# An early-fusion network of two layers: attention of layer 0 on folded matrices, other passes for its norms, and a new order of all stages

## The reference

```python
h = patchify(x) @ W + b                              # 16 batches of 36 image tokens, 64 channels
h = concat([h, table[x_txt] + pe], axis=1)           # and 512 text tokens: 548 tokens a batch
# layer 0, attention
u = layernorm(layernorm(h)) * g + b                  # the second with gain and bias
Q, K, V = u @ wq + bq, u @ wk + bk, u @ wv + bv
R = layernorm(h) + relu(Q @ K.T / 8) @ V
h = h + layernorm(R + relu(R @ w1 + b1) @ w2 + b2) * fg + fb
# layer 0, MoE: 8 experts, each token to its best, at most 1.25 * T / 8 tokens an expert
z = layernorm(h); probs = softmax(z @ gate_w + gate_b)
h = h + prob_best * kept * (relu(z @ w1[e] + b1[e]) @ w2[e] + b2[e])
# layer 1, attention over channels: 16 heads of 4, k and v normalised in each head
z = layernorm(h); q, k, v = split(z @ W_qkv.T + b_qkv)
a = gelu((q @ (k.T @ v / 548) + z) @ W_proj + b_proj) + z
h = h + a
# layer 1, MoE: each token through all 8 experts, the two best weighted
z = layernorm(h); w = top2(softmax(z @ Wr + br))
h = h + sum_e w_e * (gelu((norm(z) * ln_g[e] + ln_b[e]) @ W1[e] + b1[e]) @ W2[e] + b2[e])
```

## Time and profile before

| | |
|---|---|
| median of 3 runs | 848.64 us (847.61 to 850.04) |
| span of the profiled execution (no other time of it is given) | 846.4 us |
| PE busy | 729.7 us, 86% |
| DVE busy | 612.2 us, 72% |
| ACT busy | 481.7 us, 57% |
| POOL busy | 433.1 us, 51% |

### The profile page before, as it was taken

How to read it: one execution, slowest core, us unless ns; L and a number is a source line. 1 busy time by engine, 2 the same in 40 slices (tenths; PEclk the granted TensorE clock), 3 DMA queues, 4 the chain that set the end, 5 groups by cost and what they waited for, 6 DMA issues and landing times.

```text
span 846.4 us, 15831 instructions
## 1 busy us (share of the span) xinstructions
PE 729.7 (86%) x4619; PEld 487.1 (58%) x4619; DVE 612.2 (72%) x2308; ACT 481.7 (57%) x980; POOL 433.1 (51%) x470
## 2 busy tenths in 40 slices
PE   3589999999988689965789989989989999899995
PEld 1366777666655257643456555556555656566672
DVE  4557899989678536576777889888888977786231
ACT  1255655555541146642246877766788666777552
POOL 5732617773764600246646667667676763223222
PEclk8599999999997889995679999999999999999988
DMA  7910000000000023220022221222221122223200
GB/s 216 359 53 9 14 8 19 22 21 5 5 4 3 4 58 97 75 66 12 6 57 57 62 56 17 57 59 63 62 63 41 31 55 61 62 62 61 62 14 7
DMA packets 60976, 43.69 MB, mean 52 GB/s; under 512 B 29100, under 2 KB 56252, under 8 KB 60636
## 3 DMA queue, kind: packets, MB, share of 16 engines
q1 hardware_dynamic: 51820, 36.35, 17.2%
q0 software_dynamic: 7200, 4.17, 2.4%
q10 hardware_dynamic: 1872, 2.18, 0.9%
HBM read 31.66 MB, written 13.47 MB: 53 GB/s over the span
## 4 chain that ended last, share of the span: by engine, by line
PE 26%; ACT 15%; DVE 14%; issue 9%; POOL 2%; DMA 1%; DVEq 0%; ACTq 0%; POOLq 0%
ACT scratch L715 7%; PE psum L628 6%; PE psum L1140 5%; PE psum L1141 4%; ACT L715 3%; PE psum L1340 3%; ACT L664 2%; PE psum L1147 2%; DVE xt L788 1%; PE psum L1322 1%; PE psum L1118 1%; PE psum L602 1%; ACT L659 1%; DVE kh L885 1%; DVE stats L1507 1%
## 5 line engine op out<-in xcount | busy, mean ns | idle before, releaser
L715 ACT ACTIVATE scratch<-psum,fb 128x512 f32<-128x512 f32 (+2 forms) x288 | 172.2, 665 | 37.4 <-PE psum L1141 36.1
L628 PE MATMUL psum<-scratch,w_fw 128*64 128x256 f32 (+2 forms) x1152 | 141.7, 383 | 11.4 <-DVE scratch L978 5.7
L538 POOL TENSOR_TENSOR prob<-prob,scratch 128x256 f32<-128x256 f32 (+2 forms) x126 | 79.3, 629 | 141.0 <-DVE scratch L978 139.4
L497 POOL DMA_INDIRECT uu<-expert_out,slot_i x80 | 83.2, 1040 | 88.3 <-issue 68.7
L1079 POOL DMA_INDIRECT slots_buf<-xt,slot_i x80 | 82.5, 1032 | 68.0 <-DVE slot_i L1754 45.8
L628 PEld LDWEIGHTS psum<-scratch,w_fw 128*64 128x64 f32 x1152 | 79.1, 140 | 56.5 <-DVE scratch L978 13.5
L1065 POOL DMA_INDIRECT emb<-in_table,w_ids x64 | 63.4, 991 | 55.8 <-DVE stats L1507 33.5
L1405 ACT ACTIVATE prob<-psum 128x292 f32<-128x292 f32 (+1 forms) x160 | 55.1, 396 | 52.2 <-PE psum L1207 52.1
L1140 PE MATMUL psum<-kh,fw_hi 128*128 128x512 f32 x176 | 80.0, 455 | 0.6 <-ACT scratch L715 0.5
L1141 PE MATMUL psum<-kh,fw_lo 128*128 128x512 f32 x176 | 71.8, 408 | 0.0
L978 DVE SCALAR_TENSOR_TENSOR scratch<-psum,w_fb,X 128x256 f32<-128x256 f32 (+1 forms) x119 | 54.4, 460 | 16.9 <-PE psum L628 15.5
(11 more groups left out here) (272 smaller groups left out, 1715.7 us busy)
## 6 DMA issues: line engine op xcount, KB each, us to landing
X<-share_buf SPq DMA_DIRECT2D x32, 512.0 KB
slots_buf<-zeros SPq DMA_DIRECT2D x8, 352.0 KB, 4.9
expert_out<-zeros SPq DMA_DIRECT2D x8, 352.0 KB, 4.9
out<-H SPq DMA_DIRECT2D x16, 128.0 KB
X<-in_patches ACTq DMA_DIRECT2D x3, 576.0 KB, 7.3
slots_buf<-xt,slot_i POOLq DMA_INDIRECT x80, 2.2
uu<-expert_out,slot_i POOLq DMA_INDIRECT x80, 2.5
emb<-in_table,w_ids POOLq DMA_INDIRECT x64
```

Source lines behind the costliest of these rows:

```text
L497: pool.indirect_dma_start(yg[b % 2][0:rows, s, :], None, expert_out, bass.IndirectOffsetOnAxis(slot_i[0:rows, b, (s + 1) % SLOTS:(s + 1) % ...
L538: pool.tensor_tensor(total[t % 2][:, 0:z], total[t % 2][:, 0:z], part[m % PARTS][:, 0:z], ALU.add).then_inc(sem("summed"), 1)
L628: last = pe.matmul(bank(6 + n % 2)[h * D:(h + 1) * D, 0:z], w["fw2"][:, e * J + j, :], hid[(J * n + j) % (J * UNITS)][:, h * z:(h + 1) * z ...
L715: act.activation(hid[m % (J * UNITS)][:, 0:z], bank(2 + m % 4)[:, 0:z], ACT.Gelu, bias=fb1[:, e * J + j:e * J + j + 1]).then_inc(sem("gelu ...
```

## The change

- `norm1b` writes the normalised tokens plus one (the mean taken is lowered by the deviation), twice: DVE writes one copy, ACT's `twin` the other beside it. Four tiles `xt` instead of two. Since the 64 channels of such a token sum to 64, a bias divided by 64 can be added to each row of a weight; so `prep` makes of query and key weights one matrix `w_u`, and of the value weights and bias `w_v`.
- `t1` turns the five slots of 128 columns (both copies) into the WIDE banks; `k_high` and `k_low` make the halves of the turned tokens themselves: they are the keys. `q` is `w_u` against both halves, four fp32r matmuls. `k`, `v`, `vals`, `stack1` are gone. `attend` multiplies the scores with the tokens, and `o_turn` is the product with `w_v`.
- `norm2a` ends with five scalar_tensor_tensor (subtract mean, times gain), one a slot; `norm2b` is the reciprocal and five scalar_tensor_tensor. `norm3b` leaves out the subtraction of the mean; the gate's weights and the experts' first weights are centred instead (`centre_w`, `centre_copy`).
- The attention weights come in one DMA (`wqkv`, 48 KB) instead of three.
- All tables of the order are new. `moe_bias` stands third on PE, `moe_gains`, `low_moe`, `high_moe`, `high_w`, `low_w` among batches 0 to 3; the gathers stand earlier, the scatters later on POOL; sixteen fills more stand at the end of stage one and the start of the experts; of the later fills ten stand behind `kv` of batch 0. `up` of the first tile stands right behind the first `route`; `kv_b` of batch 0 stands before `mixed` of batch 1.

```diff
             def t1(b):
-                banks.take(pe, TURN, sem("xs1"), b + 1)
-                pe.wait_ge(sem("norm1b"), (b + 1) * PER["norm1b"] - 1)
-                turn_pairs(pe, xt[b % 2], 0).then_inc(sem("t1"), 1)
+                banks.take(pe, WIDE, sem("k_low"), b + 1)
+                pe.wait_ge(sem("twin"), b + 1)
+                for s in range(SLOTS):
+                    rows, at0 = P if s < TXT else N_IMG, s // 2 * P
+                    last = pe.transpose(bank(2 + s % 2)[:, at0:at0 + rows], xt[b % XT][0:rows, s].rearrange("p k c -> p (k c)"), ident[0:rows, 0:rows])
+                last.then_inc(sem("t1"), 1)
...
             def q(b):
-                q_or_k(b, "wq")
-            def k(b):
-                q_or_k(b, "wk")
-            def v(b):
-                slots_by(pe, bank(7), xs1[b % 2], w["wv"]).then_inc(sem("v_prod"), 1)
+                banks.take(pe, WIDE, sem("q_low"), b + 1)
+                pe.wait_ge(sem("k_low"), b + 1)
+                for h, z in enumerate(SIDES):
+                    pe.matmul(bank(2 + h)[:, 0:z], w_u[:], kh[b % 2][:, h * ODD:h * ODD + z], start=True, stop=False)
+                    last = pe.matmul(bank(2 + h)[:, 0:z], w_u[:], kl[b % 2][:, h * ODD:h * ODD + z], start=False, stop=True)
+                last.then_inc(sem("q_prod"), 1)
...
-                turn_back(pe, ot[b % 2], 1).then_inc(sem("o_turn"), 1)
+                slots_by(pe, bank(1), ot[b % 2], w_v).then_inc(sem("o_turn"), 1)
...
+            def centre_w(c):
+                pe.matmul(bank(0), centre[:], ew1[0:D, c * 512:(c + 1) * 512], start=True, stop=True).then_inc(sem("centre_prod"), 1)
...
+            def twin(b):
+                act.wait_ge(sem("norm1b"), b * PER["norm1b"] + 5)
+                if b >= XT:
+                    act.wait_ge(sem("t1"), b - XT + 1)
+                act.activation(xt[b % XT][:, :, 1, :], xt[b % XT][:, :, 0, :], ACT.Identity).then_inc(sem("twin"), 1)
...
             def norm1b(b):
+                st(dve.tensor_tensor(mean1[:], mv1[b % 2][:, :, 0], sd1[b % 2][:, 1, :], ALU.subtract))
...
+                st(dve.tensor_tensor(zt[:], H[:, b], bc(mean1[:], D), ALU.subtract))
+                st(dve.tensor_tensor(ratio1[:], sd1[b % 2][:, 1, :], rs[:, 0, :], ALU.mult))
+                st(dve.tensor_tensor(x, zt[:], bc(rs[:, 1, :], D), ALU.mult))
+                st(dve.scalar_tensor_tensor(out=X[:, b], in0=x, scalar=-1.0, in1=bc(ratio1[:], D), op0=ALU.add, op1=ALU.mult))
...
             def norm2a(b):
+                for s in range(SLOTS):
+                    st(dve.scalar_tensor_tensor(out=uu[b % 2][:, s, :], in0=uu[b % 2][:, s, :], scalar=mv2[b % 2][:, s, 0:1], in1=w["fg"][:], op0=ALU.subtract, op1=ALU.mult))
...
             def norm2b(b):
-                st(dve.tensor_tensor(zt[:], uu[b % 2][:], bc(mv2[b % 2][:, :, 0], D), ALU.subtract))
-                st(dve.tensor_tensor(zt[:], zt[:], bc(rs[:, 0, :], D), ALU.mult))
-                st(dve.tensor_tensor(zt[:], zt[:], bs(w["fg"][:], SLOTS), ALU.mult))
-                st(dve.tensor_tensor(H[:, b], H[:, b], zt[:], ALU.add))
+                for s in range(SLOTS):
+                    st(dve.scalar_tensor_tensor(out=H[:, b, s, :], in0=uu[b % 2][:, s, :], scalar=rs[:, 0, s:s + 1], in1=H[:, b, s, :], op0=ALU.mult, op1=ALU.add))
...
             def norm3b(b):
-                st(dve.tensor_tensor(zt[:], H[:, b], bc(mv3[b % 2][:, :, 0], D), ALU.subtract))
-                st(dve.tensor_tensor(xt3[b % XT3][:, 0:SLOTS, :], zt[:], bc(rs[:, 0, :], D), ALU.mult))
+                st(dve.tensor_tensor(xt3[b % XT3][:, 0:SLOTS, :], H[:, b], bc(rs[:, 0, :], D), ALU.mult))
```

More of the change, by code:

```diff
@@ L57 @@
 FMAX = 3.4028234663852886e38
-PER = dict(norm1a=11, norm1b=4, qk_low=3, vals=1, resid=1, norm2a=11, norm2b=5, norm3a=10, norm3b=3, gate=6, place=7,
+PER = dict(norm1a=11, norm1b=6, resid=1, norm2a=16, norm2b=6, norm3a=10, norm3b=2, gate=6, place=7,
            mixed=12, weighted=5, norm4=3, kvnorm=3, fold=3, resid2=11, norm5=4, route_a=11, route_b=6)
@@ L259, in early_fusion_kernel @@
[L259 to L263, removed]
+        POOL_ONE = ((-50.75, "gather_a"), (-38.625, "gather_b"), (84.5, "offset"), (320.75, "scatter_a"), (354.25, "scatter_b"))
@@ L264, in early_fusion_kernel @@
+        DVE_ONE = ((2.25, "norm1a"), (44.5, "norm1b"), (109.625, "k_low"), (123.375, "q_low"), (183, "resid"), (229.375, "norm2a"),
+                   (241.625, "norm2b"), (245.625, "norm3a"), (254.25, "norm3b"), (262.375, "gate"), (277.098, "place"))
         MOE, DOWN_LAG, GELU_LAG, WEIGH_LAG, SUM_LAG, BACK_LAG, FINISH_LAG = 170, 1.5, 0.75, 2.5, -0.5, 12.75, 12
@@ L1171, in _ @@
             pe.wait_ge(sem("early_in"), EARLY_IN)
-            pe.matmul(bank(7)[:, 0:1], w["wq"][0:D, 0:P], w["norm_b"][:], start=True, stop=True)
-            pe.matmul(bank(7)[:, 1:2], w["wk"][0:D, 0:P], w["norm_b"][:], start=True, stop=True)
-            pe.matmul(bank(7)[:, 64:64 + D], w["norm_b"][:].to_broadcast([D, P]), w["wv"][0:D, 0:D], start=True, stop=True).then_inc(sem("bias_prod"), 1)
+            pe.wait_ge(sem("affine"), 1)
+            turned = [aff[:, m].rearrange("p k c -> p (k c)") for m in range(3)]
@@ L1629, in q_low @@
                 lo = by_side(qst[b % 2][D:P, :], RIGHT)
-                dve.scalar_tensor_tensor(out=lo, in0=both(2)[D:P], scalar=bq[D:P, 0:1], in1=lo.bitcast(F32), op0=ALU.add, op1=ALU.subtract).then_inc(sem("qk_low"), 1)
-            def k_low(b):
-                dve.wait_ge(sem("qk_high"), 2 * b + 2)
-                hi, lo = by_side(kh[b % 2][:], RIGHT), by_side(kl[b % 2][:], RIGHT)
-                dve.scalar_tensor_tensor(out=lo, in0=both(2), scalar=bk[:, 0:1], in1=hi.bitcast(F32), op0=ALU.add, op1=ALU.subtract).then_inc(sem("qk_low"), 2)
@@ L1637, in vals @@
[L1637 to L1641 removed]
+                dve.tensor_tensor(lo, both(2)[D:P], lo.bitcast(F32), ALU.subtract).then_inc(sem("q_low"), 1)
             def resid(b):
@@ L1755, in place @@
                 st.close()
-            table = dict(resid=resid, q_low=q_low, norm1a=norm1a, norm2a=norm2a, gate=gate, norm3b=norm3b, k_low=k_low, vals=vals, norm1b=norm1b, norm2b=norm2b,
+            table = dict(resid=resid, q_low=q_low, norm1a=norm1a, norm2a=norm2a, gate=gate, norm3b=norm3b, k_low=k_low, norm1b=norm1b, norm2b=norm2b,
                          place=place, norm3a=norm3a, prep=prep, late_weights=late_weights, moe_gains=moe_gains, low_moe=low_moe)
```

492 lines of the change are left out of this document (376 added, 116 removed), and 113 rows, old and new, of tables (ACT_MOVED, DVE_MOVED, PE_MOVED).

## The result

The changed kernel takes 799.42 us (median of 4 runs, 798.7 to 799.72) against 849.34 us of the kernel before (4 runs): a ratio of 0.941, 95% interval 0.939 to 0.943. That is 50 us less where 27.5 were forecast. The profiled executions have spans of 797.9 and 846.4 us, 48.5 us apart.

| milestone | before, us | after, us | gained in this stretch |
|---|---|---|---|
| first copy of attended tokens | 48.45 | 54.53 | -6.1 |
| the copy of batch 15 | 249.89 | 241.15 | 14.8 |
| last placing | 286.72 | 273.74 | 4.2 |
| first product of the experts | 298.51 | 286.63 | -1.1 |
| kv bias of batch 0 | 379.08 | 359.47 | 7.7 |

What follows compares the result with a forecast made beforehand. Stage one was taken as bound by PE and DVE together, layer 1 mainly by PE. From 848.64 us: -15 pace, -6.5 stage-one end, 0 start, +1 between stages, -4 and -3 stage two, -27.5 to 821; range 797 to 838, own 811 to 827.

Steps and rivals of the forecast that it cites:

- Pace of stage one: Stage one, per batch: DVE relieved by 1.0 us and PE by 1.75, pace 13.43 to 12.4, -15 us over 15 batches.
- norm 2: DVE in stage one: ten 128x64 pieces at 0.15 us replace four passes, -0.45 us a batch, bounds -0.5 and +0.8.
- the pace follows the smaller relief: Stage one: with PE and DVE both full, the pace falls by DVE's 1.0 us a batch, not PE's 1.75.
- rival C: Stage one: norm 2's pieces cost 0.28 us each, pace stays DVE-bound at 13.4, -15 is lost, 836 us; chance 0.07.
- the sign that DVE would be fuller than PE: Stage one: DVE fuller than PE in the new profile, listed among what would show the forecast.
- Once-only work: MoE bias folding, gains and low half move from stage one's end to batches 0 to 3: -5.5 us, costed at nothing there.
- Between the stages: Before the experts: clock-keeping matmuls after the last count grow from 30 to 60, +1 us, bounds 0 and +5.
- Stage two: Layer 1 beside its MoE, steady part: new order, no work removed, 14 more table loads; -3 us, between -25 and +18.
- the -4 at the head: Start of stage two: kv of batch 0 first, up product a batch earlier, fills clumped; -4 us, bounds -12 and +6.
- Rival B: Stage two: new order closes PE's idle time, 22.7 to 23.7 us a batch instead of 25, total 799 to 810; chance 0.22.
- My own sign of being wrong: Layer 1: pitch outside 24.0 to 25.2 us a batch; also stage one paced by POOL or a chain of waits.
- Rival D: Stage two slower: clumped fills and earlier MoE leave PE thin at the head, loads delay gelus; 852 us, chance 0.08.

Runs made afterwards that it cites:

- The experiment in the old order: The changed kernel with stage one in the order of the kernel before, new steps fitted into the old places; 883.01 us, ratio 1.040.
- the exchanges: All four engines' stage-two lists and fills swapped: changed kernel with the old order, 833.15 us; kernel before with the new order, 812.87 us.
- the three moves that I tried alone: Kernel before, two weighings earlier on DVE: 890.94 us; kernel before, square later on ACT: 862.87 us; changed kernel, square earlier on ACT: 810.74 us.
- theory 1: Expectation of 789 to 793 us for the changed kernel with the last bias added by DVE instead of POOL; measured 797.0 us.

## Why the forecast was right in direction, and too small

**Pace of stage one.** Forecast 12.4 us, -15; measured 12.44, -14.8. The number held, but its terms did not, so that it held is luck. Between the copies of batches 5 and 14 DVE works 109.8 us before and 105.7 after, 12.20 and 11.75 us a batch: a relief of 0.45 instead of 1.0. The term that was mis-sized is norm 2: the pieces take 0.21 each, 1.07 us for five twice, against my 0.15, so the exchange gives +0.2 instead of -0.45 (my bounds were -0.5 and +0.8), and with it my sum would be -0.34. In this stretch the pace fell by 1.03 us (13.79 to 12.76); the other half is idle time of DVE, 1.6 us a batch before and 1.0 after, for which the forecast had no term. That the pace follows the smaller relief of work is therefore not what happened: the batches got shorter by more than DVE's relief and by less than PE's, which is 1.4 us (13.20 to 11.77) and not 1.75. The order is the likely giver of the other half; no run separates it. That rival C would make the pace 13.4 was wrong all the same, and so was the sign that DVE would be fuller than PE (92.2 and 92.5).

**The arithmetic needs its order.** I took the pace from the engines' sums and a chain of waits only as a way to be wrong. The experiment in the old order shows that chain at 18.3 us a batch, with the new steps at the places I gave them. This was not in the forecast. The old arithmetic in the new order of stage one was not run.

**Once-only work.** Forecast -5.5 up to the last placing and, with -1 for scatters and +1 for fills, 0 from there to the experts; measured -4.2 and +1.1. It was costed at nothing at the start, and that failed: 2.07 us for each of four centring products, where I had taken 0.5 from a bf16 matmul of as many columns, and three of them on the way of batch 0. The bias products take 6.96 us instead of the 4.37 of before (granted clock 0.50 from 23 to 30 us, 0.83 at 266.5 to 271 before), but lie in PE's wait for q's low half. The first copy came 6.1 us late (bound +4). It mattered little: without this work the total is 1.9 us less.

**Between the stages.** +1 forecast, 1.1 measured; 60 at 0.24 each end at 286.8, and against thirty they hold the experts' first product back by 2.3 us. What they keep is the clock in the experts (1.00 instead of 0.83 from 280 to 300 us), worth 1.9 of that.

**Stage two.** The step that failed is "between -25 and +18 I take -3, near nothing, for no work is removed", with the -4 at the head. Measured: -7.7 at the head (bound -12), 0.0 until batch 5, and -28.9 from there to the end. The -7.7 lie between the experts' first product and the first kv bias, where I had 0 for the experts; PE works 70.2 us there instead of 74.9, at a clock of 1.00 instead of 0.97. For all of it the exchanges give 34 and 36 us. Rival B was this case, 22.7 to 23.7 us a batch for 14 to 25 us; it got 0.22, and the pitch measured is 23.4. My own sign of being wrong, a pitch outside 24.0 to 25.2, came with it. The argument against it, that only 9 of PE's 23 idle us had one cause, counted waits by the last releaser. PE's idle time had several releasers, and the order of all four lists took it from 25.4 to 14.8 us in eleven batches; the other 7.2 us of the gain there are busy time that shrank with the same products. Which entries do it stays open: the three moves that I tried alone, two in the old order and one in the new, each made the kernel slower, by 11 to 42 us, and neither of those in the old order hit the changed place exactly.

**Table loads.** 14 more were forecast and 14 came: 74 loads of 1.283 us in the trace against 60. ACT's share in the ten batches rose from 73 to 84%, and PE waited 4 us in them for gelus (L1466 2.7, L954 1.3), so most of the 18 us was hidden. By the Trainium skill ("ScalarE: Activation LUTs", section "What ACT_TABLE_LOAD costs") a drain of about 1.38 us would come on top of each; no run here shows it, since in the changed kernel too the next operation (566.66 us) starts 1.29 us after the load began (565.37). Rival D had part of its condition (a clump of fills, a clock of 0.50 from 380 to 400 us, the loads) but not its price.

**Range.** 799.4 lies in 797 to 838, near its edge, and outside the forecast's own 811 to 827. That it lies inside owes something to two misses that partly cancel: stage one with the passage to the experts was forecast at -20.5 and gave -11.9, stage two at -7 and gave -36.6. With stage one as forecast the time would have been some 791 us, below the range.

## What to carry over

Where a kernel's engines run written-out lists, take the idle time of the bottleneck in a steady stage as a gain that a new order can reach for, even if no wait has a large share of it (here it took 10.6 of 25.4 us), and the same lists as what can make new arithmetic pay or lose; sum the engines' work only after the chain through shared banks has been checked against the pitch. Don't count on winning it place by place: the three single moves tried here took 11, 14 and 42 us away. Once-only work at a start costs its price at the clock that the trace shows there, but ask whether a later batch pays it back before you count it.

## Unexpected on the hardware

- Five scalar_tensor_tensor of 128x64 fp32 with a scalar from memory take 1.07 us, 0.21 each, where five statistics of the same shape take 0.73 (0.15 each).
- Some DVE instructions that overlap POOL's addition of 128x320 are longer by 1.0 to 1.4 us: 128x120 in 1.64 instead of 0.28 us (163.89, POOL's at 164.46 for 0.91), five of 128x64 in 2.32 and 2.39 instead of 1.07. They are those with both inputs in SBUF. The low halves, which read PSUM, keep their 0.77 us beside it (82.59, 95.33 and 107.11), and the statistics their 0.21 (150.54, 174.54). With that addition on DVE the kernel won 2.4 us of the 6 to 10 that theory 1 gave.
- An fp32 matmul of 64x128 by 512 columns takes 2.07 us, recorded as two instructions, at the low clock (granted 0.50 from 30 to 40 us).
- With thirty clock-keeping matmuls more ahead of the experts the granted clock from 280 to 300 us is 1.00 instead of 0.83.
